# A last stage of two joined attentions: narrow heads in the text stage's form, wide keys and values on row tiles, keys first in the step

## The chip, the cores and the metric

The program runs on one core of a Trainium2 chip. The metric is the device time of one execution in microseconds (us), the median of several runs. The engines are named as the profile names them: PE (matmuls; PEld is its weight loads), DVE, ACT, POOL, and SP, which issues DMAs.

## The reference

`x` is 32 batches of 128 tokens by 128 features, `ctx_768` 32 batches of 128 tokens by 96. Four layers follow each other: L0 (layer norm, self attention, cross attention, gated feed-forward), L1 (narrow cross attention and feed-forward), L2 (wide cross attention) and L3 (narrow cross attention). The change concerns L2 and L3:

```python
# L2: 16 heads of 64
h = _layernorm(x, gamma, beta)
Q = (h @ Wq).reshape(B, NQ, 16, 64)
K = (context @ Wk).reshape(B, NC, 16, 64)
V = (context @ Wv).reshape(B, NC, 16, 64)
attn = softmax(einsum('bihd,bjhd->bhij', Q, K)) * 64 ** -0.5
x = x + einsum('bhij,bjhd->bihd', attn, V).reshape(B, NQ, 1024) @ Wo + bo
# L3: 16 heads of 8
q, k, v = x @ Wq.T, context @ Wk.T, context @ Wv.T        # 128 features
attn = softmax(einsum('bhqd,bhkd->bhqk', q, k) * 8 ** -0.5)
x = einsum('bhqk,bhkd->bhqd', attn, v) @ Wo.T + bo + x
```

All numbers are 32-bit floats. A batch needs nothing of another batch.

## The kernel before

The program has five stages, one behind the other, with a barrier after each: the two attentions of L0 (0 to 746 us), L0's feed-forward (to 858), L1's attention, called the text stage here (`text_attention`, L934, to 1031), L1's feed-forward (to 1099), and L2 with L3 in one stage (`wide_and_narrow`, L1266, to the end). `x` stays in SBUF throughout, and so does `ctxT`, the contexts turned so that features lie on partitions.

The last stage is a software pipeline over steps t of which each does one batch's worth of everything, for different batches. Each engine has its own list of a step's work, written by hand: PE's is `step` at L1629, ACT's at L1808, DVE's at L2017, POOL's at L2131, SP's behind L2157. In step t PE does, in this order: wide scores of batch t+1 in two halves (`w_score`, L1431; each half 32 passes on two row groups into two banks), weighing of the wide values of t-1 (`w_weigh`, L1518), half the queries and half the keys of t+2 (`project_T`, L1481), the first half of the transposes of the narrow probabilities of t-3 (`n_transpose_probs`, L1471), the wide output projection of t-1 (L1564), the narrow scores of t-2 (`n_score`, L1454), the other transposes, the transposed inverses (L1548), the other halves of queries and keys with the transposed narrow rows of t-1 between, the narrow weighing of t-3 (`n_weigh`, L1535), the narrow queries and keys of t-1, the transposed wide rows of t+3, the wide values of t+1 in two halves (`w_values`, L1507, 512 columns each) with the narrow output projection of t-3 between, and the narrow values of t-2.

Results of PE go through eight PSUM banks. Four (`scores`) hold the wide scores and, at other times of the step, the narrow ones. The other four are a ring: `order` (L1271) lists the 20 fills of a step as (name, batch offset, engine that empties it); the n-th fill of the program goes to bank n mod 4, and PE waits (`start_fill`, L1422) until the fill four places earlier has been emptied. So the order of this list, the order of PE's list and those of ACT and DVE must fit each other.

The softmax of a wide batch: DVE takes row maxima of a half's scores (L1882), ACT exponentiates the first eight heads head by head with the maximum as bias and sums on the way (`w_exponentiate_0`, L1686); for the other eight DVE subtracts and ACT exponentiates all at once (L1710), DVE sums. POOL multiplies by the inverse sums (`w_divide`, L2125). To turn the probabilities, DVE transposes them in squares of 32 by 32 (`w_turn_squares`, L1947), and SP moves the squares to DRAM and back to their turned places (`away` and `back`, L2160 and L2168, called the relay here). The narrow softmax has the same form with its own maxima, exponentials and sums, and PE turns its probabilities; the inverses are turned too and multiplied in as the weighed result is evicted.

Steps 4 to 27 are a loop of four steps each turn (`TURN`, L1277); the rest is written out. The last wide batch has its own step (L1587), with its probabilities turned by PE, and the steps after it a list of their own (`tail_step`, L1608).

The text stage does narrow attention of the same size (16 heads of 8) in another form, written out without a loop. Scores are computed twice: once with queries on partitions for the maxima alone (L1017, two matmuls of 256 columns per row group), and once turned, with keys on partitions (L1029, four of 128 columns), where the negated maxima, turned by PE (L1050) and appended to the queries by DVE (L1202, L1204), make the product come out less its maximum. ACT exponentiates the turned scores, four operations of 512 columns (L1126), and these are already in the form that the weighing (L1061) needs. A column of ones in the values gives the sums, and the division follows after the weighed result is turned back.

Loads of weights go through SP (`load`, L187); those of L2 are issued at the end of the first stage's program (`later_loads`, L226, at t == 2 * BATCHES), by `load_wide` (L199) in five DMAs of whole tensors.

## Time and profile before

| | us |
|---|---|
| median of 3 runs (lowest, highest) | 1674.45 (1668.0, 1679.09) |
| the profiled execution | 1676.32 |
| its span | 1674.6 |
| mean granted clock of TensorE | 0.99 |
| last stage | 1099 to 1674.6 |

Busy shares of the span: PE 97%, PEld 81%, DVE 75%, ACT 70%, POOL 42%. The span runs from the first to the last recorded instruction; the execution's own time is 1.7 us longer.

In rows of a timeline an entry holds consecutive instructions of one line and kind, with their number behind the x; its duration runs to the modelled end of the last, so that the next entry of the same engine can start a little before it ends. PEclk is the share of full speed that TensorE was granted.

### The profile page before, as it was taken

How to read it: one execution, taken by the hardware profiler on the slowest of the kernel's cores; microseconds unless marked ns; L12 is line 12 of the kernel's file. 1: busy time of each engine (PE TensorE's matmuls, PEld its weight loads, DVE VectorE, ACT ScalarE, POOL GpSimd, SP SyncE). 2: the span in 40 equal slices, each digit the busy share in tenths (PEclk: the TensorE clock that was granted, in tenths of full speed). 3: DMA queues.
4: the chain of work that ended last, by engine and by line, in shares of the span. 5: the costliest groups of instructions: out<-in, count | busy, mean ns of one | idle time of the engine just before them, and what ended most of it. 6: DMA issues, size and time to landing. Idle time of an engine off the chain costs nothing. (4 is left out here: it accounts for less than half of the span.)

```text
span 1674.6 us, 48052 instructions
## 1 busy us (share of the span) xinstructions
PE 1620.9 (97%) x16480; PEld 1348.4 (81%) x16480; DVE 1252.0 (75%) x2424; ACT 1174.7 (70%) x3648; POOL 704.6 (42%) x1027
## 2 busy tenths in 40 slices
PE   7999999999999999989999998988999999999998
PEld 5788888888888888879978887876888888888876
DVE  4877777777777777757767775656888888888885
ACT  4777777777777777743336665455888888888886
POOL 3444444454444444332224442643343444444441
PEclk9999999999999999999999999998999999999999
DMA  6777777788667776740000000014343444344440
GB/s 185 202 190 189 185 189 191 201 217 218 186 183 199 184 186 182 202 135 1 0 2 3 3 3 2 0 40 138 120 142 119 141 120 139 121 139 121 139 130 9
DMA packets 225246, 211.60 MB, mean 126 GB/s; under 512 B 19475, under 2 KB 222805, under 8 KB 225109
## 3 DMA queue, kind: packets, MB, share of 16 engines
q1 hardware_dynamic: 225108, 209.92, 45.4%
q8 instruction: 67, 1.10, 0.3%
q14 instruction: 71, 0.57, 0.1%
HBM read 109.72 MB, written 100.14 MB: 125 GB/s over the span
## 5 line engine op out<-in xcount | busy, mean ns | idle before, releaser
L907 POOL TENSOR_TENSOR L_probs<-L_probs,L_inv_sum 128x1024 f32<-128x1024 f32 x128 | 242.8, 1897 | 87.2 <-DVE L_inv_sum L803 87.2
L691 ACT ACTIVATE L_probs<-L_scores,L_neg_max 128x128 f32<-128x128 f32 x512 | 182.8, 386 | 135.0 <-DVE L_neg_max L783 135.0
L777 DVE TENSOR_REDUCE L_row_max<-L_scores 128x8 f32<-128x1024 f32 x128 | 156.2, 1220 | 41.8 <-PE L_scores L549 41.8
L2128 POOL TENSOR_TENSOR L2L_w_probs<-L2L_w_probs,L2L_w_inv_sum 128x1024 f32<-128x1024 f32 x64 | 121.4, 1896 | 124.2 <-DVE L2L_w_inv_sum L1931 123.7
L809 DVE STREAM_TRANSPOSE L_squares<-L_probs 128x1024 f32<-128x1024 f32 x125 | 153.0, 1224 | 0.3 <-POOL L_probs L907 0.3
L549 PE MATMUL L_scores<-L_kT,L_qT 64*128 64x128 f32 x2048 | 131.8, 278 | 0.9 <-ACT L_kT L680 0.9
L600 PE MATMUL L_ring<-L_probsT,L_v 128*64 128x128 f32 x2048 | 126.6, 276 | 3.9 <-issue 1.8
L600 PEld LDWEIGHTS L_ring<-L_probsT,L_v 128*64 128x64 f32 x2048 | 110.5, 137 | 23.9 <-issue 19.6
L549 PEld LDWEIGHTS L_scores<-L_kT,L_qT 64*128 64x128 f32 x2048 | 119.4, 188 | 12.5 <-ACT L_oT L680 8.1
L793 DVE TENSOR_REDUCE L_sums<-L_probs 128x8 f32<-128x1024 f32 x64 | 78.1, 1220 | 64.8 <-ACT L_probs L698 64.8
L1195 DVE TENSOR_REDUCE L_maxima<-L_s_banks 128x4 f32<-128x512 f32 x128 | 87.5, 688 | 44.6 <-PE L_s_banks L1017 44.6
L1695 ACT ACTIVATE L2L_w_probs<-L2L_scores,L2L_w_neg_max 128x128 f32<-128x128 f32 x256 | 90.4, 371 | 41.7 <-DVE L2L_w_neg_max L1895 41.7
L691 ACT ACTIVATION_READ_ACCUMULATOR L_probs<-L_scores,L_neg_max 128x1 f32 x512 | 115.8, 226 | 0.0
L680 ACT ACTIVATE L_oT<-L_ring 128x512 f32<-128x512 f32 x128 | 76.5, 599 | 39.7 <-PE L_ring L600 39.6
L1884 DVE TENSOR_REDUCE L2L_w_row_max<-L2L_scores 128x8 f32<-128x1024 f32 x64 | 76.7, 1198 | 28.8 <-PE L2L_scores L1450 28.8
L1706 ACT ACTIVATE L2L_n_probs<-L2L_scores,L2L_n_neg_max 128x128 f32<-128x128 f32 x256 | 90.7, 377 | 4.8 <-DVE L2L_n_neg_max L1901 4.1
L1253 POOL TENSOR_SCALAR L_k_apart<-L_qk,quad_mask 128x128 f32<-128x128 f32 x116 | 50.3, 448 | 93.2 <-ACT L_qk L1153 93.2
L680 ACT ACTIVATE L_kT<-L_ring 128x512 f32<-128x512 f32 x128 | 76.8, 600 | 18.2 <-PE L_ring L557 18.2
L2104 POOL TENSOR_TENSOR L2L_n_x_bias<-L2L_n_rows_h,bias_L 128x128 f32<-128x128 f32 x32 | 14.6, 456 | 177.9 <-DVE x L1980 177.8
L680 ACT ACTIVATE L_qT<-L_ring 128x512 f32<-128x512 f32 x128 | 76.2, 595 | 17.3 <-PE L_ring L557 12.0
L1126 ACT ACTIVATE L_exps<-L_t_banks 128x512 f32<-128x512 f32 x128 | 69.4, 597 | 19.7 <-PE L_t_banks L1029 19.7
L1684 ACT ACTIVATE L2L_n_probsT<-L2L_ring 128x512 f32<-128x512 f32 x128 | 70.4, 611 | 17.9 <-PE L2L_ring L1477 17.9
(236 smaller groups left out, 4578.7 us busy)
## 6 DMA issues: line engine op xcount, KB each, us to landing
L_relay<-L_squares SPq DMA_DIRECT2D x125, 512.0 KB, 3.4
L_probsT<-L_relay SPq DMA_DIRECT2D x500, 128.0 KB, 3.7
L2L_relay<-L2L_w_squares SPq DMA_DIRECT2D x62, 512.0 KB, 3.4
L2L_w_probsT<-L2L_relay SPq DMA_DIRECT2D x248, 128.0 KB, 2.9
out_x<-x SPq DMA_DIRECT2D x32, 64.0 KB, 2.7
L0a_wq<-in_L_xattn_Wq SPq DMA_DIRECT2D x2, 256.0 KB, 2.9
L0a_wk<-in_L_xattn_Wk SPq DMA_DIRECT2D x2, 256.0 KB, 3.2
L0a_wv<-in_L_xattn_Wv SPq DMA_DIRECT2D x1, 512.0 KB, 6.3
```

Source lines behind the costliest of these rows:

```text
L549: last = nc.tensor.matmul(scores[:, s, r, i, :], q[part, i, at.n % 2, :], k[part, i, at.n % 2, :], start=True, stop=True, tile_position=(h ...
L600: last = nc.tensor.matmul(to[WIDE * r:WIDE * (r + 1), TOKENS * i:TOKENS * (i + 1)], v[:, at.n % 2, WIDE * h:WIDE * (h + 1)], probsT[:, at. ...
L680: nc.scalar.activation(to, src, ACT.Copy).then_inc(emptied["act"], 1)
L691: done = nc.scalar.activation(slot_probs(at, 0)[:, n, :], scores[:, 0, r, i, :], ACT.Exp, scale=layer_of(at).scale, bias=neg_max[:, n:n + ...
L777: nc.vector.tensor_reduce(row_max[:, s, :], slot(s), AX.X, ALU.max).then_inc(max_ready[s], 1)
L793: nc.vector.tensor_reduce(sums[:, :, 1, :], slot_probs(at, 1).rearrange("p (r i) k -> p r i k", r=2), AX.X, ALU.add).then_inc(sum_ready, 1)
L809: nc.vector.transpose(squares[:, at.n % 2, :, SLOT_HEADS * s:SLOT_HEADS * (s + 1), :] .rearrange("p j h a -> p h j a"), slot_probs(at, s). ...
L907: nc.gpsimd.tensor_tensor(to, to, inv_sum[:, :, s, :].unsqueeze(3) .to_broadcast([TOKENS, 2, GROUP, TOKENS]), ALU.mult).then_inc(divided, 1)
L1195: nc.vector.tensor_reduce(maxima[:, b % 2, g, :, 0:1].rearrange("p j d -> p (j d)"), s_bank(b, g), AX.X, ALU.max, negate=True).then_inc(ma ...
L1695: done = nc.scalar.activation(w_slot(at, 0)[:, h, :], scores[:, 0, r, i, :], ACT.Exp, scale=W.scale, bias=w_neg_max[:, h:h + 1], accum_out ...
L1706: done = nc.scalar.activation(n_slot(at, 0)[:, h, :], scores[:, 0, r, i, :], ACT.Exp, scale=N.scale, bias=n_neg_max[:, h:h + 1], accum_out ...
L2128: nc.gpsimd.tensor_tensor(to, to, w_inv_sum[:, :, s, :].unsqueeze(3) .to_broadcast([TOKENS, 2, GROUP, TOKENS]), ALU.mult).then_inc(w_divid ...
```

## The change

- The stage is written out whole: no loop, no special last or tail steps. Where batch 31's probabilities are turned by PE, this stands at the front of step 32.
- The ring has 22 fills a step in another order, shown below.
- Wide keys and values are computed on row tiles. The 96 context features are three blocks of 32 rows, and the inner columns are split in four; each of PE's four row groups has one quarter of the columns, and adds up three products of 32 rows. For this the context lies four times in a new tile, `ctx_blocks` (one copy for each row group, 16 batches at a time), written to DRAM and loaded back by SP during the text stage, with later chunks of 8 batches loaded at steps 8 and 16. The weights lie in the same form, loaded in 24 DMAs instead of two. ACT empties keys and values as four copies of 256 columns each, where it made two of 512.
- In PE's list the keys of batch t+2 stand first, ahead of both halves of the wide scores of t+1.
- The narrow attention takes the text stage's form. Its scores are issued in two calls a step, `n_both_scores`; each interleaves the scores for the maxima of two row groups (batch t-2) with those less the maxima of the two other row groups (batch t-3).
- POOL sets the narrow parts (six operations of 128 columns), and takes the layer norm's normalisation from DVE; ACT takes the eviction of the turned wide rows from DVE. POOL no longer copies rows and contexts.
- At the stage's start DVE clears two tiles, 2,560 columns in all, where it cleared one of 1,280.

```diff
-    order = [("w.PV0", -1, "act"), ("w.PV1", -1, "act"), ("w.q0", 2, "act"), ("w.k0", 2, "act"),
-             ("n.T0", -3, "act"), ("n.T1", -3, "act"), ("w.Wo", -1, "dve"), ("n.T2", -3, "act"), ("n.T3", -3, "act"),
-             ("n.iT", -3, "act"), ("w.q1", 2, "act"), ("n.hT", -1, "act"), ("w.k1", 2, "act"), ("n.PV", -3, "dve"),
-             ("n.qk", -1, "act"), ("w.hT", 3, "dve"), ("w.v0", 1, "act"), ("n.Wo", -3, "dve"), ("w.v1", 1, "act"),
-             ("n.v", -2, "act")]
+    order = [*((f"w.k{g}", 2, "act") for g in CHUNKS_4), ("n.mT", -3, "dve"), ("w.PV0", -1, "act"),
+             ("w.PV1", -1, "act"), ("n.PV", -4, "act"), ("w.q0", 2, "act"), ("n.D", -4, "dve"), ("w.Wo", -1, "dve"),
+             *((f"w.v{g}", 0, "act") for g in CHUNKS_4), ("n.hT", -1, "act"), ("n.oT", -4, "act"),
+             ("w.q1", 2, "act"), ("n.qk", -1, "act"), ("n.v", -3, "act"), ("n.Wo", -4, "dve"), ("w.hT", 3, "act")]
...
+                for g in range(4):
+                    for r in range(CTX // 32):
+                        load(sp, "L2", W["L2", "k"][32 * g:32 * (g + 1), r, :, :], keys[g][:, r, :, :])
+                        load(sp, "L2", W["L2", "v"][32 * g:32 * (g + 1), r, :], values[g][:, r, :])
...
+            def n_both_scores(t, s_groups, t_groups):
+                for h in range(2):
+                    if real(t - 2):
+                        for g in s_groups:
+                            n_score_for_max(t - 2, g, h)
+                    if real(t - 3):
+                        for j in (2 * h, 2 * h + 1):
+                            for g in t_groups:
+                                n_score_less_max(t - 3, g, j)
...
+            def w_keys(b):
+                ctx_blocks.await_loaded(pe, b)
+                to = [start_fill(f"w.k{g}", b) for g in CHUNKS_4]
+                for c in range(2):
+                    for r in range(3):
+                        for g in CHUNKS_4:
+                            part = slice(QUAD * g, QUAD * (g + 1))
+                            last = nc.tensor.matmul(to[g][:, TOKENS * c:TOKENS * (c + 1)], W.wk[part, r, c, :],
+                                                    ctx_blocks.of(b)[part, r, :], start=r == 0, stop=r == 2,
+                                                    tile_position=(QUAD * g, 0))
...
+            def w_values(b):
+                to = [start_fill(f"w.v{g}", b) for g in CHUNKS_4]
+                for r in range(3):
+                    for g in CHUNKS_4:
+                        part = slice(QUAD * g, QUAD * (g + 1))
+                        last = nc.tensor.matmul(to[g][:, 0:INNER // 4], ctx_blocks.of(b)[part, r, :], W.wv[part, r, :],
+                                                start=r == 0, stop=r == 2, tile_position=(QUAD * g, 0))
```

PE's list of a step after, without the tests of whether a batch exists:

```diff
+            for t in range(first, last + 1):
+                    w_keys(t + 2)
+                    w_score(t + 1, 0)
+                    w_score(t + 1, 1)
+                    n_transpose_maxima(t - 3)
+                    w_weigh(t - 1, 0)
+                    w_weigh(t - 1, 1)
+                    n_weigh(t - 4)
+                    w_queries(t + 2, 0)
+                    n_turn_back(t - 4)
+                    w_project_out(t - 1)
+                n_both_scores(t, (0, 1), (2, 3))
+                    w_values(t)
+                n_both_scores(t, (2, 3), (0, 1))
+                    n_transpose_h(t - 1)
+                    n_transpose_o(t - 4)
+                    w_queries(t + 2, 1)
+                    n_queries_keys(t - 1)
+                    n_values(t - 3)
+                    n_project_out(t - 4)
+                    w_transpose_h(t + 3)
```

The lists of ACT and DVE follow suit. ACT's: four copies of keys, exponentials of the first four heads, copies of the weighed wide values (two of 512 columns), of `n.PV` and `w.q0`, exponentials of the next four heads and of the second half (1024 columns), two narrow exponentials of 512 columns, four copies of values, `n.hT`, `n.oT`, two narrow exponentials, `w.q1`, `n.qk`, `n.v`, `w.hT`. DVE's: row maxima of half 0, their negation, inverses, row maxima of half 1, the subtraction, the append of the narrow maxima (which empties `n.mT`), squares, statistics, the narrow division (empties `n.D`), the wide finish, inverses, narrow maxima of two groups, sums, narrow maxima of two groups, squares, the narrow finish. The waits of PE's new parts:

```diff
+            def w_score(b, s):
+                await_emptied(pe, f"w.q{s}", b)
+                if s == 0:
+                    for g in CHUNKS_4:
+                        await_emptied(pe, f"w.k{g}", b)
+                    if real(b - 4):
+                        pe.wait_ge(n_max_ready, 4 * (b - 4) + 4)
...
+                elif real(b - 5):
+                    pe.wait_ge(n_exp_ready, 4 * (b - 5) + 4)
...
+            def n_score_for_max(b, g, h):
...
+                    if g >= 2:
+                        pe.wait_ge(n_max_ready, 4 * b + g - 1)
+                    elif real(b + 3):
+                        pe.wait_ge(w_exp_ready[0], 2 * (b + 3) + 2)
...
+            def n_score_less_max(b, g, j):
...
+                    await_emptied(pe, "n.mT", b)
+                    if g < 2:
+                        pe.wait_ge(n_exp_ready, 4 * b + g + 1)
+                    elif real(b + 4):
+                        pe.wait_ge(w_shifted, b + 5)
```

## Rows read from the trace of the kernel before

**Rows 1.** Windows of the last stage: head, 26 steps, tail, a stretch of the head.
```profile
core 0: us, PE busy (x) PEld busy (x) DVE busy (x) ACT busy (x) POOL busy (x), PEclk, DMA share, GB/s
1101.00:1183.06 82.06, 70.26 (x620) 56.04 (x618) 53.26 (x98) 50.78 (x173) 30.03 (x44) 0.92 0.34 103
1183.06:1617.54 434.48, 431.87 (x4758) 363.40 (x4757) 374.85 (x644) 380.40 (x1327) 183.71 (x258) 1.00 0.44 131
1617.54:1674.60 57.06, 45.99 (x507) 36.18 (x506) 33.95 (x59) 40.99 (x139) 13.44 (x18) 0.94 0.14 42
1160.40:1167.20 6.80, 6.52 (x23) 4.24 (x25) 3.25 (x5) 4.75 (x17) 1.33 (x2) 0.50 0.52 157
```

**Rows 2.** Timeline of PE, one steady step: start, duration, engine, line, operation, operands.
```profile
1417.39 2.06 PE L1450 MATMUL L2L_scores<-L2L_w_kT,L2L_w_qT 64*128 64x128 f32 x32
1419.38 1.97 PE L1529 MATMUL L2L_ring<-L2L_w_probsT,L2L_w_v 128*64 128x128 f32 x32
1421.27 1.16 PE L1484 MATMUL L2L_ring<-L2L_w_hT,L_wq 128*128 128x128 f32 x8
1422.27 1.06 PE L1484 MATMUL L2L_ring<-L2L_w_cT,L_wk 96*128 96x128 f32 x8
1423.16 1.04 PE L1477 MATMUL L2L_ring<-ident,L2L_n_probs 128*128 128x128 f32 x8
1424.04 1.95 PE L1569 MATMUL L2L_ring<-L_wo,L2L_w_oT 128*128 128x128 f32 x16
1425.92 1.14 PE L1467 MATMUL L2L_scores<-L2L_n_k_apart,L2L_n_qT 32*128 32x512 f32 x8
1426.99 1.09 PE L1477 MATMUL L2L_ring<-ident,L2L_n_probs 128*128 128x128 f32 x8
...
1430.02 1.08 PE L1542 MATMUL L2L_ring<-L2L_n_probsT,L2L_n_v 128*32 128x128 f32 x32
1431.15 0.48 PE L1503 MATMUL L2L_ring<-L2L_n_hT,L_wqT 128*128 128x128 f32 x2
...
1431.81 1.02 PE L1509 MATMUL L2L_ring<-L_wv,L2L_w_cT 96*128 96x512 f32 x2
1432.66 0.39 PE L1575 MATMUL L2L_ring<-L_woT,L2L_n_oT 128*128 128x128 f32 x2
```

**Rows 3.** Timeline of PE in the text stage, from the turned maxima on.
```profile
944.39 0.33 PE L1050 MATMUL L_b_bank<-ident,L_maxima 128*128 128x128 f32 x1
944.64 1.08 PE L1061 MATMUL L_a_bank<-L_exps,L_v 128*32 128x128 f32 x32
945.66 0.48 PE L1017 MATMUL L_s_banks<-L_k_apart,L_q_part 32*128 32x256 f32 x2
...
946.22 0.39 PE L1029 MATMUL L_t_banks<-L_q_part,L_k_apart 32*128 32x128 f32 x4
...
946.44 0.39 PE L1029 MATMUL L_t_banks<-L_q_part,L_k_apart 32*128 32x128 f32 x4
946.76 0.33 PE L1074 MATMUL L_a_bank<-ident,x 128*128 128x128 f32 x1
```

**Rows 4.** Groups by line, text stage, weight loads: busy us, mean ns, idle before.
```profile
L1029 PEld LDWEIGHTS L_t_banks<-L_q_part,L_k_apart 32*128 32x128 f32 x864 | 52.6, 186 | 0.3 <-issue 0.2
```

**Rows 5.** Timeline of DVE, text stage and the steady step of rows 2.
```profile
945.05 0.34 DVE L1202 SCALAR_TENSOR_TENSOR L_q_part<-L_b_bank,L_half_mask,L_q_part 128x128 f32<-128x128 f32 x1
...
945.57 0.68 DVE L1195 TENSOR_REDUCE L_maxima<-L_s_banks 128x4 f32<-128x512 f32 x1
...
1418.60 1.23 DVE L1884 TENSOR_REDUCE L2L_w_row_max<-L2L_scores 128x8 f32<-128x1024 f32 x1 [0.78 <-PE L2L_scores L1450]
```

**Rows 6.** Timeline of ACT in the same step.
```profile
1420.17 0.37 ACT L1695 ACTIVATE L2L_w_probs<-L2L_scores,L2L_w_neg_max 128x128 f32<-128x128 f32 x1 [1.02 <-DVE L2L_w_neg_max L1895]
...
1421.55 1.09 ACT L1684 ACTIVATE L2L_w_oT<-L2L_ring 128x512 f32<-128x512 f32 x2
```

**Rows 7.** Waits of SP's queue, 690 to 780 us: in total, times, longest.
```profile
SPq L385 <- PEq L385: 10.8, 1, 10.8
```

**Rows 8.** Timeline of SP at the end of the first stage, one issue of a load.
```profile
733.31 0.43 SPq L187 DMA_DIRECT2D L_wq<-in_L_xattn_Wq  x1
```

1153 lines of the change are left out of this document (471 added, 682 removed).

## The prediction

> **What bounds the kernel now.** I read the table of windows first, one row per stretch of the last stage [rows 1]. Its row from 1183.06 to 1617.54 us runs from the wide scores that step 4 issues to those of step 30, so it holds 26 steps: 434.48 / 26 = 16.71 us each. PE is busy for 431.87 of the 434.48, DVE for 374.85, ACT for 380.40, POOL for 183.71. So PE alone sets the step, and the other engines keep up with it. Then the timeline of PE over one of these steps [rows 2]: groups follow each other without a gap, and from start to start the scores take 1.99 us, the weighing of wide values 1.89, a half of the queries 1.00, a half of the keys 0.89, two fills of transposed narrow probabilities 0.88, the wide output projection 1.88, the narrow scores 1.07, the narrow weighing 1.13, half of the wide values 0.85. Eight passes of 128 columns in 0.88 make 0.11 a pass. The head of the stage (82.06 us) has PE busy for 70.26 at a mean clock of 0.92, with stretches such as 1160.40 to 1167.20 at 0.50, the 1.2 GHz level; the tail takes 57.06 us [rows 1].
>
> The profiled execution took 1676.32 us (span 1674.6), the median of the three runs is 1674.45. The sum is made against 1676.32; at the median's level everything stands 2 us lower. A measurement of this kernel tells about 1% (17 us) from no change.
>
> **What leaves PE in a step** [rows 2]: four fills of narrow transposes 2 x 0.88, the transposed inverses (one pass, 0.11), keys 2 x 0.89, values 2 x 0.85, narrow scores 1.07, narrow weighing 1.13: 7.55.
>
> **What comes.** The text stage already runs the narrow form that is taken over, and its timeline prices it [rows 3]: transposed maxima 0.25, weighing 1.02 (944.64 to 945.66), one call of both kinds of scores 1.10 (945.66 to 946.76), of which the change issues two: 2.20. Turning back is two passes, 0.22, turning the output one, 0.11. Wide values by row tiles are 12 matmuls of 256 columns; as a matmul is two passes (the 4 of a half of the queries stand as x8), this is 24 passes in 6 sets of four row groups, each at twice 0.11: 1.30. Wide keys are 24 matmuls of 128 columns, 48 passes in 12 sets. No row shows this shape. If a set costs one pass it is 12 x 0.11 = 1.32, and nothing goes below that. By the text stage's weighing (32 passes on four tiles at a time in 1.02, 0.032 a pass) it is 1.53. By a call of both scores (24 passes on four row groups in 1.10, 0.046 a pass) it is 2.2. I take 1.42, between the two nearest, and keep 2.2 for the range. Another change of tile shape costs 0.1 (the narrow weighing of before took 1.13, the text stage's 1.02). Sum: 0.25 + 1.02 + 2.20 + 0.22 + 0.11 + 1.30 + 1.42 + 0.1 = 6.6. PE's work falls by about 1 us a step, to 15.5 where each group is counted on its own.
>
> How weights come in decides about the keys. In a call of both scores the scores less maxima run on two row groups, x4 at 946.22 and x4 at 946.44 [rows 3]: two passes for each row group in 0.22, though one load of weights there lasts 186 ns [rows 4]. So a row group takes its next weights at the pace of its passes. The Trainium skill, "TensorE: Matmul & The Clock Gate", Part 3 (The mechanism, what overlaps and what doesn't), says that a weight load overlaps running matmuls only when its row group differs; with all four row groups busy, as in the new keys, each set would then wait for its own loads. These rows don't bear that out for two row groups of four; for a set on all four no row here speaks. What it would make of the time is the third rival.
>
> **What then waits.** I walked a steady step in order: each engine's list as the diff has it, durations of rows, 0.2 us from PE's last pass to its reader (half of the scores is done 1.0 after 1417.39, and the reduce of it starts at 1418.60 [rows 2, 5]), about 0.1 between other engines; neighbours on an engine overlap a little, so on ACT 512 columns cost 0.48, 256 some 0.27, four exponentials with sums 1.38 (1420.17 to 1421.55 [rows 6]). Time 0 is the first half of the wide scores.
> - Scores end at 1.99, transposed maxima at 2.18, wide weighing at 4.08, narrow weighing at 5.1. The queries then want the bank of the transposed maxima, four fills back. DVE appends those only behind both row maxima and the subtraction: 1.25 + 1.26 + 0.23 + 1.20 + 1.14 = 5.08, and the append is two operations, 0.6 [rows 5]. PE waits 0.6.
> - Queries from 5.7, turning back, output projection to 8.85. The first call of both scores needs ACT's second half of the exponentials, behind the copy of the queries: 0.1. After the values the second call waits for the maxima of the first two groups, two reduces of 0.61 to 0.68 on DVE [rows 5]: 0.25.
> - The transpose of the next wide rows goes to the bank of the second half of the queries. ACT copies that behind four copies of values, two turned blocks and two exponentials of 512 columns, until about 14.8: 0.3.
> - The keys stand first in the next step and want the last four banks at once. The latest is that transpose's, which ACT empties behind two other copies: 0.5. Nothing of PE's lies between the two, so nothing covers it.
>
> Work 15.5 and waits 1.75 give a step of 17.25 us. With the keys at 1.32 the walk gives 17.15, at 1.53 17.35, at 2.2 about 18.0. Its softest term is the handoff: with none at all the step is 16.4, with handoffs half as long again 17.8.
>
> **Other engines.** ACT loses the narrow exponentials' accumulations and the copies of turned probabilities and comes to 10.9 us a step in the walk, DVE to 11.8, POOL to 8.2 (it takes over the normalisation and sets the narrow parts): below the step, so they matter by their order alone. The relay through DRAM starts from DVE's squares as before; in the walk a landing 2 us later moves nothing. Twice in the steady steps SP issues a chunk of context, 12 x 0.43 = 5 us [rows 8], between relays: inside that slack or nearly, 0 to 3 us each; I take 0.
>
> **Before the stage.** At the end of the first layers SP issues 22 more loads: 22 x 0.43 = 9.5 us [rows 8], against 10.8 that SP waited there for PE [rows 7]. I take 0; if pieces issue more slowly than whole tensors, up to 6 show. The text stage gets one write and 24 loads on an SP without other work: 0.
>
> **Head and tail.** The walk gives the head 76 us, with memsets of 2,560 columns ahead of the first statistics (the 1024-wide reduce takes 1.23 [rows 5], so about 1.5 more than for the 1,280 columns of before). Of the 82.06 at a mean clock of 0.92, some 6.6 are lost clock [rows 1]. The new head idles too, so I let half of that come back: -3 (-7 to +1). In the tail the last batch's turned probabilities stay about the same work and the narrow chain is one lag longer: +3 (0 to +5).
>
> **Sum**: 26 x (17.25 - 16.71) = +14, -3, +3: +14 on 1676.3, at the median's level 1674.45 + 14 = 1688.5, so 1689.
>
> **Rivals.**
> - *Packed PE.* The waits come from my handoffs, and ACT and DVE run early enough. For it: PE was packed before and is packed in the text stage [rows 2, 3]. Against: the append can't pass the subtraction in DVE's list. A step of 15.6: 26 x (15.6 - 16.71) = -29, head -3, tail +3: 1645. With waits of half the size (16.4): 1668.
> - *Keys at the rate of single passes, slower.* At 0.046 a pass, as in both scores, the keys take 2.2, all of it bare at the step's front: 18.0, +34: 1708. It decides where the group takes over 1.9. For it: the row of both scores; against: the row of the weighing [rows 3].
> - *Keys waiting for their loads, slower.* A set's loads start when its row groups are free: 12 x (0.186 + 0.11) = 3.6 [rows 3, 4], a step of 19.4, +70: 1746. Against: the beat of 0.22 above. This is the Trainium skill's rule of "TensorE: Matmul & The Clock Gate", Part 3.
> - *Clock.* Waits now recur in every step, and in the head (11.8 us of idle in 82) rows at 0.50 follow [rows 1]. A drop of 3.4 us in each step costs 1.7: +44 more, 1733. Against: each new wait is at most 0.6.
> - *It doesn't do what it says.* The row groups run one after another, so keys and values cost 48 x 0.11 and 24 x 0.22, 10.6 instead of 2.7: past 1850. Against: the call of both scores [rows 3].
>
> **Chances.** Forecast with its handoffs (1672 to 1705): 0.57. Packed or half packed: 0.16. Keys at the rate of single passes: 0.17. Waiting for loads 0.03, clock 0.06, no overlap 0.01. The likeliest is 1689. To hold 8 in 10 the range goes from 1658 (takes in the half-packed case) to 1712 (the keys at 2.2). Slower by over 1% (over 1691.2): the last four rivals, 0.27, and the upper part of the forecast's own range, 0.15: 0.42. Faster by over 1% (under 1657.7): most of the first rival, 0.14. Within 1%: 0.44.
>
> **What would show it.** In the profile of the changed kernel: 17.25 us from scores to scores; PE busy near 90% of the steady window where it was 99%; idle ahead of the first queries laid to DVE's append (0.6), ahead of the keys to ACT's copy of the turned rows (0.5), and ahead of that transpose (0.3); the keys 1.3 to 1.5 from start to start. The walk is wrong if PE is packed, the tiles' price if the keys take 2 us, and the rest if the first layers end later or the steady window's clock is under 1.00.

## The result, and the profile after

| | before | after |
|---|---|---|
| median of 4 runs each, us | 1674.43 | 1714.74 |
| lowest to highest | 1668.0 to 1679.09 | 1711.64 to 1719.87 |
| ratio after to before, 95% interval | | 1.0246 (1.0213 to 1.028) |
| the profiled execution / its span | 1676.32 / 1674.6 | 1719.87 / 1718.1 |

The change makes the kernel slower by 2.5%, 40 us. The forecast was 1689, the range ended at 1712. The windows of the last stage after, cut at the same events as [rows 1] (head from the first statistics to the wide scores of step 4, 26 steps, tail):

```profile
core 0: us, PE busy (x) PEld busy (x) DVE busy (x) ACT busy (x) POOL busy (x), PEclk, DMA share, GB/s
1111.44:1191.70 80.26, 63.58 (x926) 56.67 (x925) 45.65 (x81) 47.22 (x161) 37.69 (x55) 0.94 0.36 112
1191.70:1651.12 459.42, 419.47 (x6767) 383.02 (x6763) 306.97 (x565) 314.31 (x1012) 223.17 (x331) 1.00 0.44 131
1651.12:1718.10 66.98, 55.79 (x717) 46.30 (x716) 25.31 (x57) 28.93 (x81) 18.65 (x33) 0.84 0.13 40
```

459.42 / 26 = 17.67 us a step; all but the last (14.98) and one other (18.48) are 17.75 (the forecast: 17.25, before: 16.71). PE is busy for 91% of it where it was 99%, at a full clock. The profiled execution is the slowest of the four, 5 us over their median. Against the profile of before its 43.5 us of span come from: the 26 steps +24.9, the tail +9.9, the head -1.8 with 0.7 more ahead of it, and 9.7 before the last stage begins, where the rest of the program is the same. Half of these 9.7 stand at the barrier after the first layers, half in the feed-forward behind it. The first 14 us of that feed-forward, before and then after:

```profile
746.00:760.00 14.00, 11.46 (x69) 10.21 (x70) 9.13 (x34) 5.27 (x10) 3.55 (x8) 1.00 0.01 1
```

```profile
751.00:765.00 14.00, 11.85 (x41) 10.24 (x42) 5.61 (x24) 3.26 (x6) 3.56 (x8) 0.53 0.14 43
```

It starts 4.9 us later (751.34 for 746.45), and then runs at a clock of 0.53, so that 41 passes are done where before there were 69. Of the 4.9 us, 1.9 are that PE's last projection ahead of the barrier starts later (745.67 for 743.74), and 3.0 that PE then waits 3.6 us where it waited 0.7. SP's timeline shows what it waits for: a load of a piece of weights, with its strides, is issued in 0.57 to 0.68 us, one in 1.11 (two stand for 24), where [rows 8] had 0.43 for a whole tensor. The 24 take 15.5 us, from 734.29 to 749.84, and SP's own wait at the barrier, 10.8 us in [rows 7], is 0.2:

```profile
734.29 0.68 SPq L188 DMA_DIRECT2D L_wk<-in_L_xattn_Wk  x1
735.02 0.58 SPq L188 DMA_DIRECT2D L_wv<-in_L_xattn_Wv  x1
```

```profile
SPq L404 <- PEq L404: 0.2, 1, 0.2
```

One steady step on PE after, to be read against [rows 2] (in brackets the idle time before an entry, and what ended it):

```profile
1421.57 1.62 PE L1509 MATMUL L2L_ring<-ctx_blocks,L_wk 32*128 32x128 f32 x48 [0.64 <-ACT L2L_w_hT L1718]
1423.12 2.06 PE L1445 MATMUL L2L_scores<-L2L_w_kT,L2L_w_qT 64*128 64x128 f32 x32
1425.11 0.33 PE L1567 MATMUL L2L_ring<-ident,L2L_n_maxima 128*128 128x128 f32 x1
1425.36 1.97 PE L1536 MATMUL L2L_ring<-L2L_w_probsT,L2L_w_v 128*64 128x128 f32 x32
1427.26 1.08 PE L1579 MATMUL L2L_ring<-L2L_n_exps,L2L_n_v 128*32 128x128 f32 x32
1428.88 1.13 PE L1497 MATMUL L2L_ring<-L2L_w_hT,L_wq 128*128 128x128 f32 x8 [0.54 <-ACT L2L_n_weighed L1669]
1429.85 0.38 PE L1590 MATMUL L2L_ring<-ident,L2L_n_weighed 128*128 128x128 f32 x2
1430.07 1.95 PE L1556 MATMUL L2L_ring<-L_wo,L2L_w_oT 128*128 128x128 f32 x16
1432.18 0.48 PE L1460 MATMUL L2L_scores<-L2L_n_k_apart,L2L_n_q_part 32*128 32x256 f32 x2 [0.17 <-ACT L2L_w_probs L1680]
...
1435.95 0.33 PE L1596 MATMUL L2L_ring<-ident,x 128*128 128x128 f32 x1
...
1437.79 0.39 PE L1617 MATMUL L2L_ring<-L_woT,L2L_n_oT 128*128 128x128 f32 x2
1438.38 0.30 PE L1562 MATMUL L2L_ring<-ident,L2L_w_rows_h 128*128 128x128 f32 x1 [0.20 <-ACT L2L_w_qT L1669]
1439.32 1.62 PE L1509 MATMUL L2L_ring<-ctx_blocks,L_wk 32*128 32x128 f32 x48 [0.64 <-ACT L2L_w_hT L1718]
```

The group of keys takes 1.55 us from start to start (1421.57 to 1423.12): 48 passes, 0.032 each, though their weight loads last 186 ns each:

```profile
L1509 PEld LDWEIGHTS L2L_ring<-ctx_blocks,L_wk 32*128 32x128 f32 x1200 | 36.5, 186 | 20.1 <-issue 20.1
```

The waits stand where the walk put them: ahead of the queries, of the first call of both scores, of the wide rows' transpose and of the keys. The bracket counts from the modelled end of the pass before; from start to start, less the passes themselves, the four are 0.60, 0.23, 0.37 and 0.83 us (the last is 1439.32 less 1438.38 and a pass of 0.11). The last is the large one. On ACT, the chain behind it:

```profile
1436.32 0.28 ACT L1669 ACTIVATE L2L_n_hT<-L2L_ring 128x128 f32<-128x128 f32 x1 [0.49 <-PE L2L_ring L1596]
...
1436.65 1.10 ACT L1690 ACTIVATE L2L_n_exps<-L2L_scores 128x512 f32<-128x512 f32 x2
1437.60 0.63 ACT L1669 ACTIVATE L2L_w_qT<-L2L_ring 128x512 f32<-128x512 f32 x1
1438.08 0.43 ACT L1669 ACTIVATE L2L_n_qk<-L2L_ring 128x256 f32<-128x256 f32 x1
1438.34 0.34 ACT L1669 ACTIVATE L2L_n_v<-L2L_ring 128x128 f32<-128x128 f32 x1
1438.72 0.46 ACT L1718 ACTIVATE L2L_w_hT<-L2L_ring,L_ln_b,L_ln_g 128x128 f32<-128x128 f32 x1
```

ACT works without a gap from the exponentials to the copy of the narrow values; the copy of the wide rows, with scale and bias, takes 0.46, where the plain copies of 128 columns take 0.28 (`n.hT`) and 0.34 (`n.v`). And ahead of the queries, on DVE (the profile names ACT's `n_weighed` for that wait, which is not in the list of what these queries wait for; the append ends at 1428.73, 0.15 before them):

```profile
1426.99 1.23 DVE L1805 TENSOR_TENSOR L2L_w_probs<-L2L_scores,L2L_w_row_max 128x1024 f32<-128x1024 f32 x1
1428.13 0.34 DVE L1846 SCALAR_TENSOR_TENSOR L2L_n_q_part<-L2L_ring,L2L_half_mask,L2L_n_q_part 128x128 f32<-128x128 f32 x1
1428.39 0.34 DVE L1848 SCALAR_TENSOR_TENSOR L2L_n_q_part<-L2L_ring,L2L_half_mask,L2L_n_q_part 128x128 f32<-128x128 f32 x1
```

### The profile page after: what moved, and what is told of

Its sections match the earlier page's. It is cut to its first block and busy times, and to the rows that moved or that the text cites. A ratio compares the mean times of both kernels' runs of the same rounds, so it can differ in the third digit from the quotient of the medians.

```text
span 1718.1 us, 51406 instructions
## 1 busy us (share of the span) xinstructions
PE 1619.2 (94%) x19008; PEld 1384.8 (81%) x19008; DVE 1168.3 (68%) x2330; ACT 1093.2 (64%) x3264; POOL 757.0 (44%) x1126
## 5 line engine op out<-in xcount | busy, mean ns | idle before, releaser
L1840 DVE TENSOR_REDUCE L2L_n_maxima<-L2L_scores 128x4 f32<-128x512 f32 x128 | 82.4, 686 | 31.0 <-PE L2L_scores L1460 31.0
L699 ACT ACTIVATE L_qT<-L_ring 128x512 f32<-128x512 f32 x128 | 76.2, 595 | 16.2 <-PE L_ring L576 10.8
L1690 ACT ACTIVATE L2L_n_exps<-L2L_scores 128x512 f32<-128x512 f32 x128 | 69.7, 602 | 25.9 <-PE L2L_scores L1476 25.9
L1497 PE MATMUL L2L_ring<-L2L_w_hT,L_wq 128*128 128x128 f32 x512 | 70.7, 282 | 14.9 <-ACT L2L_n_weighed L1669 13.4
L1460 PE MATMUL L2L_scores<-L2L_n_k_apart,L2L_n_q_part 32*128 32x256 f32 x512 | 77.7, 396 | 6.4 <-ACT L2L_w_probs L1680 4.4
```

The costliest lines, as they stand in the source:

```text
L699: nc.scalar.activation(to, src, ACT.Copy).then_inc(emptied["act"], 1)
L1460: last = nc.tensor.matmul(s_bank(g)[:, 2 * (1 - h):2 * (1 - h) + 2, :], n_q_part[part, b % 2, h, :], n_k_apart[part, b % 2, 2 * h:2 * h + ...
L1497: last = nc.tensor.matmul(to[:, TOKENS * c:TOKENS * (c + 1)], W.wq[:, BANK * n + 128 * c:BANK * n + 128 * (c + 1)], w_hT[:, b % 2, :], sta ...
L1690: nc.scalar.activation(n_exps[:, b % 2, GROUP * g:GROUP * (g + 1), :].rearrange("p h q -> p (h q)"), t_bank(g).rearrange("p j q -> p (j q) ...
```

## The experiments

Each kernel is the changed one with the edit named, unless said otherwise. "Step" is the usual time from wide scores to wide scores in the trace, "tail" from the scores of the last wide batch to the end. The kernel before was run again beside each group, and the ratios are to it: 1675.42 us beside the first four experiments, 1671.91 beside the next four, 1675.52 beside the next three, 1675.29 beside the last three. So whole times of different groups can stand 3.6 us apart by that alone. Tails and heads are from one profile each.

**The 24 loads moved into the text stage.**

```diff
         def first_context_blocks(sp):
...
+            for g in range(4):
+                for r in range(CTX // 32):
+                    load(sp, "L2", W["L2", "k"][32 * g:32 * (g + 1), r, :, :], keys[g][:, r, :, :])
+                    load(sp, "L2", W["L2", "v"][32 * g:32 * (g + 1), r, :], values[g][:, r, :])
             ctx_blocks.write(sp, ctxT)
```

> Edit: the 24 loads of the wide weights' row tiles are issued by SP at the start of the text stage, where SP has nothing else to do, in place of the end of the first stage. Theory A (SP's issue time holds the barrier after the first stage by 4.9 us, and the idle PE then starts the feed-forward at half clock, 4.8 us more): the feed-forward's first statistics come back to 746.4 us from 751.3, its first 20 us run at a clock of 1.00, and the whole is 9 to 10 us shorter than the changed kernel, near 1705. Rival B (the loads themselves, 24 short transfers, collide with the feed-forward): the barrier comes 4.9 us earlier, the other 4.8 us move to the text stage, near 1710. Rival C (the clock drop there is chance): 4.9 us and no more.

Measured: 1710.03 us, ratio 1.0206 (1.0183 to 1.0229), step 17.75. The feed-forward starts at 745.0 and its first 14 us run at full clock:

```profile
745.00:759.00 14.00, 11.89 (x73) 10.63 (x74) 9.40 (x37) 5.25 (x10) 3.56 (x8) 1.00 0.00 1
```

So the loads held the barrier. In all six profiles with the loads in the old place SP waits 0.2 us there and PE 3.4 to 4.9; in the ten others, the kernel before among them, SP waits 10.7 to 14.3 and PE 0.7. What the clock adds is not settled. From the feed-forward's first statistics to the text stage's first memset the changed kernel's profile shows 98.9 us, and 94.1 is the time at full clock. The five others with the loads in the old place show 95.2 to 95.9. But so do four of the ten that have no such wait, 95.6 to 95.8, among them the kernel with four edits below:

```profile
750.00:764.00 14.00, 11.90 (x58) 10.20 (x59) 7.95 (x30) 5.21 (x10) 3.56 (x8) 0.88 0.00 1
```

So up to 1.7 us are lost there without the wait too, and the 4.8 that theory A adds stand in one profile only. The last stage begins 11.1 us earlier than in the changed kernel's profile, where theory A wanted 9 to 10, but the medians differ by 4.7, and the intervals of the two ratios overlap. For the whole that is nearer to rival C.

**The wide rows turned earlier.** PE's transpose, ACT's copy and the ring's entry move together:

```diff
-             ("w.q1", 2, "act"), ("n.qk", -1, "act"), ("n.v", -3, "act"), ("n.Wo", -4, "dve"), ("w.hT", 3, "act")]
+             ("w.hT", 3, "act"), ("w.q1", 2, "act"), ("n.qk", -1, "act"), ("n.v", -3, "act"), ("n.Wo", -4, "dve")]
```

> Edit: the transpose of the wide rows of batch t+3 and its copy stand ahead of the second half of the queries, no longer at the end of the step; the ring's list follows. Theory A (the keys wait bare for the chain transpose, copy on ACT, release, 0.94 us from transpose to keys, and the transpose itself waits 0.37 for the bank of the queries): the keys then wait for the copy of the narrow values and for DVE's last operation alone, some 0.3 to 0.5 us after PE's last projection; the step falls from 17.75 to 17.0 to 17.2, the whole by 15 to 23 us. Rival B (ACT's list as a whole is late at the end of the step, whatever stands last): the wait stays with another name, the step within 0.2 of 17.75. Rival C (the keys are slow because of their weight loads): the group of keys keeps 1.55 us, as in A, so B and A are told apart by the step alone.

Measured: 1712.42 us, step 17.70. Rival B. The wait ahead of the transpose is gone, but the keys now wait 1.0 us by the bracket, where it was 0.64, and for another copy, the last one that ACT makes:

```profile
1431.82 0.39 PE L1617 MATMUL L2L_ring<-L_woT,L2L_n_oT 128*128 128x128 f32 x2
1433.19 1.62 PE L1509 MATMUL L2L_ring<-ctx_blocks,L_wk 32*128 32x128 f32 x48 [0.99 <-ACT L2L_n_v L1669]
```

Here the keys wait for the last copy of ACT's list, whichever it is.

**The append earlier on DVE.**

```diff
+                if real(t - 3):
+                    n_append_maxima(t - 3)
                 if real(t + 1):
                     w_row_maxima(t + 1, 1)
                     w_subtract_maxima(t + 1)
-                if real(t - 3):
-                    n_append_maxima(t - 3)
```

> Edit: in DVE's list the append of the narrow maxima stands ahead of the second row maxima and the subtraction. Theory A (the queries wait 0.54 us for the bank that this append empties): that wait is gone, and what hangs on it follows; the step falls by 0.4 to 0.55 us to 17.2 to 17.35, the whole by 11 to 14 us. Rival B (the profile's name for that wait, ACT's copy of the narrow weighed values, is the true one): the wait of 0.54 stays and the step with it, at 17.75. Rival C (the subtraction, 0.5 us later, delays the second exponentials and with them the narrow scores): the gain is given back at the first call of both scores, whose idle time grows from 0.17 to 0.6.

Measured: 1701.36 us, ratio 1.0151 (1.0126 to 1.0176), step 17.17, shorter by 0.58 (two steps are longer, 18.02 and 18.04). The waits of PE over 1187.8 to 1633.8 us (in total, times, longest) no longer have the queries (L1497), and the other three are as they were:

```profile
PE L2L_ring L1509 <- ACT L2L_w_hT L1718: 16.0, 25, 0.6
PE L2L_ring L1562 <- ACT L2L_w_qT L1669: 5.0, 25, 0.2
PE L2L_scores L1460 <- ACT L2L_w_probs L1680: 4.5, 26, 0.2
```

Theory A, with a gain just over its range; the releaser that the profile named was not the true one.

**Keys and values at full height**, the rest as changed:

```diff
...
+            def w_keys(b):
+                for n in range(2):
+                    to = start_fill(f"w.k{n}", b)
+                    for c in range(4):
+                        last = nc.tensor.matmul(to[:, TOKENS * c:TOKENS * (c + 1)],
+                                                W.wk[0:CTX, BANK * n + 128 * c:BANK * n + 128 * (c + 1)],
+                                                ctxT[0:CTX, b, :], start=True, stop=True)
...
```

> Edit: wide keys and values at full height again (96 rows, two fills of 512 columns each, straight from the turned contexts), in the same places of the step; the narrow form and the rest stay as changed, and the loads, the blocks of contexts and their DMAs go. Theory A (row tiles save PE little and cost waits: keys on four row groups want four banks at once): PE's work grows by 0.3 for the keys and 0.4 for the values, the keys' wait of 0.64 goes (their banks are those of narrow projections, emptied earlier), so the step comes to 17.4 to 17.8, and the 9.7 us ahead of the stage come back: 1695 to 1707 in all. Rival B (row tiles are the cause of the longer step): the step falls under 17.0, the whole under 1690. Rival C (row tiles are what keeps the step short): the step is over 18.2.

Measured: 1709.65 us, step 17.98: between the forecasts, and the whole just over theory A's 1695 to 1707. The wait ahead of the keys is gone, yet the step is 0.23 longer, so PE's work grew by more than the 0.7 expected; the row tiles do shorten the step. The whole is not longer, since the first layers end without delay (745.8) and the head takes 73.8 us, 6.5 less. What shortens the head by so much was not tried.

**The last two exponentials at the end of ACT's list.**

```diff
-                if real(t - 3):
-                    n_exponentiate(t - 3, 0)
-                    n_exponentiate(t - 3, 1)
                 if real(t + 2):
                     w_queries(t + 2, 1)
...
                     w_turned_h(t + 3)
+                if real(t - 3):
+                    n_exponentiate(t - 3, 0)
+                    n_exponentiate(t - 3, 1)
```

> Edit: on ACT the last two narrow exponentials of a step (512 columns each) stand at the end of its list, behind the copies of the second queries, the narrow projections and the wide rows. The earlier transposing of the wide rows left the step at 17.71 us and the keys waiting 1.0 us for the last copy on ACT, so theory A now reads: ACT's list from these exponentials on is the chain that ends last, whatever is copied last. It predicts that the copy of the queries starts some 0.4 us earlier, PE's transpose of the wide rows no longer waits, and the keys start 0.35 us earlier: a step of 17.3 to 17.45, the whole 8 to 11 us shorter than the changed kernel. Rival B (the handoff transposes, copy, keys alone sets it, 0.94 us after the transpose whenever that comes): the step stays over 17.65. Rival C (the exponentials are missed by the next narrow weighing or the next scores): a new wait there of 0.3 us or more, and a step over 17.75.

Measured: 1709.07 us, step 17.43, shorter by 0.32, and the wait ahead of the transpose is gone: the step follows theory A. The medians fell by 5.7 only. In the profiles, 10.9 us apart, the 26 steps give 8.4, while the tail is 1.2 longer (68.2) and the head 2.7; the rest lies ahead of the stage, where the two kernels are the same.

**Keys behind both halves of the wide scores.**

```diff
-                if real(t + 2):
-                    w_keys(t + 2)
                 if real(t + 1):
                     w_score(t + 1, 0)
                     w_score(t + 1, 1)
+                if real(t + 2):
+                    w_keys(t + 2)
```

> Edit: the keys stand behind both halves of the wide scores in PE's list, and their copies on ACT behind the exponentials of the first four heads; the ring's list stays. Theory A (at the front of the step nothing covers the keys' wait): the scores follow the last projection without it, the keys find their four banks empty, and the wait of 0.64 us goes; a new one comes behind the keys, where the transposed maxima want the first keys' bank, which ACT empties only behind the exponentials (0.4 to 0.9). Step 17.0 to 17.4. Rival B (the place of the keys is worth nothing, what is won at the front is lost there in full): 17.65 to 17.85. Rival C (the front was the better place): over 17.9.

Measured: 1710.22 us, step 17.64: Rival B, a hair under its range. The wait at the front is gone, and the transposed maxima behind the keys wait for the copy of the keys (now behind the exponentials on ACT):

```profile
1412.13 1.62 PE L1509 MATMUL L2L_ring<-ctx_blocks,L_wk 32*128 32x128 f32 x48
1414.73 0.30 PE L1567 MATMUL L2L_ring<-ident,L2L_n_maxima 128*128 128x128 f32 x1 [0.98 <-ACT L2L_w_kT L1669]
```

The place of the keys is worth 0.1 us a step as long as the lists of ACT and DVE stay.

**Four edits at once**: the loads, the earlier append, the earlier transpose of the wide rows, the late exponentials.

> Edit: four at once: the 24 loads in the text stage, the earlier append, the wide rows' transpose ahead of the second queries, and the two exponentials at the end of ACT's list. Theory A (waits of ACT's and DVE's order make the step longer than before, PE's own work is 15.6): without the wait for the append and without ACT's late chain the step is 16.2 to 16.8, and the whole, with 5 to 10 us for the loads, 1668 to 1685. Rival B (PE's own work is longer than 15.6, the waits hide behind it): the step stays over 17.0 with no wait left that is worth naming. Rival C (a new chain, through the narrow exponentials or the relay, takes over): over 17.0 with one wait of more than 0.5 us.

Measured: 1684.1 us, ratio 1.0058 (1.0038 to 1.0078), step 16.61: theory A. Alone the three edits of order gave 0.58, 0.05 and 0.32, or 0.95, together 1.14. That the transpose is worth more once ACT's list no longer ends late would explain the rest; no run leaves it out of the three, so this is not shown. PE's waits, 1300 to 1600 us, two of them:

```profile
PE L2L_ring L1509 <- DVE x L1863: 8.6, 18, 0.5
PE L2L_scores L1460 <- ACT L2L_w_probs L1680: 3.1, 18, 0.2
```

Two steps of the 26 are longer, 17.64 and 18.24. Its tail:

```profile
1616.86:1686.00 69.14, 56.78 (x717) 46.87 (x716) 25.43 (x57) 29.98 (x82) 18.74 (x33) 0.81 0.13 39
```

**As that, with products of the identity in the tail** (`keep_clock(nc, to[:, 0:TOKENS], ident, 2)`, or 4, on the bank that is filled next, ahead of the waits of turning back, weighing, turning the output and projecting).

> Edit: as the kernel with four edits, and in the narrow parts of the last five batches PE multiplies the identity with itself (two or four products, into a bank that it fills next) ahead of four waits. It adds work whose result is overwritten. Theory A (the tail's 67 us, against 57 before, hold some 12 us of half clock from about 35 us before the end, where before it was 3.4): with PE kept busy the half-clock stretches shrink to some 10 us and the tail is 4 to 8 us shorter than that of the kernel without. Rival B (the tail is a chain of handoffs between ACT, DVE and PE, and the clock matters little to it): the clock rises and the time stays within 2 us. Rival C (the added products lie on the chain): 2 to 6 us longer.

Measured: 1688.39 us. The clock of the tail rises from 0.81 to 0.98, and the tail is 70.3 us against 69.1: inconclusive, since the 128 added passes, at 0.11 us each, take about 14 us on PE, in part in place of waits (its busy time in the tail grows by 7.3).

**The narrow finish ahead of the squares on DVE**, on top of the four edits:

```diff
+                if real(t - 4):
+                    n_finish(t - 4)
                 if real(t + 1) and t + 1 != LAST_WIDE:
                     w_turn_squares(t + 1, 0)
-                if real(t - 4):
-                    n_finish(t - 4)
```

> Edit: the kernel with four edits, and in DVE's list the narrow finish, which empties the bank of the narrow output projection, stands ahead of the last squares of the step. Theory A (with four edits the keys still wait 0.5 us, now for this bank, which DVE empties behind squares of 1.24 us): the finish comes 0.3 us earlier, the keys with it, the step falls from 16.72 to 16.35 to 16.5, the whole by 6 to 10 us against the four edits' 1684. Rival B (ACT's copy of the narrow values comes as late): the wait changes its name and the step stays over 16.65. Rival C (the squares, and with them the relay, come too late): a wait of the weighing of wide values for the landing.

Measured: 1687.88 us. The usual step stays at 16.61 and the wait ahead of the keys at 0.5: theory A falls. It is the handoff from the last projection through DVE to the keys, which want that bank and have nothing ahead of them. Rival C came in part: two steps are 20.9 and 22.4 us long. SP issues 12 loads of context in one go, and the relay of the next squares stands behind them; with the four edits alone the same loads cost 1.0 and 1.6 us, and here the last squares of the step also start later (0.2 us ahead of the keys, where it was 1.9). SP's timeline, and PE's at the second of the two:

```profile
1394.38 6.47 SPq L2035 DMA_DIRECT2D ctx_blocks<-ctx_turned  x12
1400.95 0.52 SPq L1983 DMA_DIRECT2D L2L_relay<-L2L_w_squares  x1
```

```profile
1410.03 1.97 PE L1536 MATMUL L2L_ring<-L2L_w_probsT,L2L_w_v 128*64 128x128 f32 x16 [2.87 <-issue]
```

Of the 5.8 us by which that step is too long, 2.9 are this wait; behind it PE is busy and runs at a mean clock of 0.58 from 1410 to 1417 us, which makes about the other half (an estimate: 7.0 x 0.42 = 2.9). In the changed kernel, with its longer step, the loads show once, as a step of 18.48 us.

**A last wide step of its own**, on top of that: the last batch's turned probabilities, weighing and output projection come in step 31 instead of 32.

```diff
+                if t == LAST_WIDE:
+                    w_transpose_probs(t, 0)
+                    w_transpose_probs(t, 1)
...
+                if t == LAST_WIDE:
+                    w_weigh(t, 0)
+                    w_weigh(t, 1)
...
+                if t == LAST_WIDE:
+                    w_project_out(t)
```

> Edit: as the kernel before it in this call, with a last wide step of its own: the last batch's probabilities are turned by PE at the end of step 31, its weighing, output projection and finish follow there, and its narrow rows are turned at the front of step 32; in the changed kernel all this stands in step 32. Theory A (the tail of 67 to 70 us against 57 is a chain of handoffs of the last batch that starts a step late; the clock that falls meanwhile is its consequence, as holding the clock changed nothing): the tail shrinks to 57 to 62 us and the whole by 7 to 12 us against the kernel before it. Rival B (the narrow form's own last steps, max, append, second scores, exponentials, division, are the tail): it stays over 65. Rival C (step 31 is so full that it gives back what is won): step 31 longer by more than 6 us, the whole within 3 us.

Measured: 1691.3 us, tail 72.1: not A, and over 65 as rival B has it. The last wide finish on DVE comes 31.4 us into the tail instead of 34.2 (first the kernel without this step, then with it):

```profile
1657.56 0.29 DVE L1835 SCALAR_TENSOR_TENSOR x<-L2L_ring,L2L_w_x_bias 128x128 f32<-128x128 f32 x1 [1.21 <-PE L2L_ring L1556]
```

```profile
1652.09 0.29 DVE L1855 SCALAR_TENSOR_TENSOR x<-L2L_ring,L2L_w_x_bias 128x128 f32<-128x128 f32 x1 [6.19 <-PE L2L_ring L1562]
```

But the last three narrow finishes then follow 11.0, 10.6 and 6.1 us apart, at half clock, where without this step they followed 8.5, 7.5 and 6.0 apart. Tail windows of the kernel without and with this step:

```profile
1623.32:1687.50 64.18, 51.21 (x717) 41.83 (x716) 26.32 (x58) 29.73 (x82) 18.64 (x33) 0.93 0.14 42
```

```profile
1620.69:1692.80 72.11, 59.89 (x717) 48.91 (x716) 26.35 (x58) 30.05 (x82) 18.65 (x33) 0.76 0.12 37
```

**Full height with these edits** (append, transpose, exponentials, finish, last wide step; no later loads).

> Edit: wide keys and values at full height, with the other edits: the earlier append, the earlier transpose of the wide rows, the late exponentials, the earlier finish and the last wide step; the loads are those of the kernel before the change. Theory A (with the waits gone, PE's own work decides, and the row tiles save 0.2 to 0.6 us of it a step): the step is 16.5 to 16.9, longer than that of the kernel with row tiles and the same edits by 0.2 to 0.5; but the head is 4 to 6 us shorter and no loads hold the first stage's end, so the whole is within 6 us of that kernel. Rival B (the row tiles cost their gain by waits): the step is shorter than with row tiles, the whole 8 us or more below it. Rival C: the step is over 17.2.

Measured: 1685.98 us, step 16.92, head 71.9, tail 71.0. Theory A, with a step just over its range. Here PE is packed again, 433.63 of 438.03 us, at the longer step:

```profile
1172.36:1610.39 438.03, 433.63 (x5444) 371.98 (x5443) 305.12 (x564) 309.93 (x906) 224.16 (x331) 1.00 0.43 130
```

This kernel shows what the row tiles are worth. Its PE at both calls of scores with the values between, then at the keys:

```profile
1400.84 0.48 PE L1456 MATMUL L2L_scores<-L2L_n_k_apart,L2L_n_q_part 32*128 32x256 f32 x2 [0.17 <-ACT L2L_w_probs L1676]
...
1405.16 0.33 PE L1584 MATMUL L2L_ring<-ident,x 128*128 128x128 f32 x1
...
1407.33 2.01 PE L1502 MATMUL L2L_ring<-ctxT,L_wk 96*128 96x128 f32 x16
1409.27 2.06 PE L1441 MATMUL L2L_scores<-L2L_w_kT,L2L_w_qT 64*128 64x128 f32 x32
```

The keys take 1.94 us here and 1.55 on row tiles, the stretch of scores and values 4.32 and 3.77: row tiles save 0.94 us of PE's time in a step. Of this 0.64 goes back, the wait of the keys for their last bank that stays with the four edits (1417.29 to 1418.15 there, less two passes of 0.11); at full height they start without a wait. What is left is the 0.31 between 16.92 and 16.61.

**The clock of the tail, with products that fit into waits.** On the four edits with the last wide step and with the context loads spread two to a step (1); on full height with the same edits, without the earlier finish (2); on the changed kernel alone (3):

```diff
+            def hold(to, b):
+                if b >= BATCHES - 4:
+                    keep_clock(nc, to[:, 0:TOKENS], ident, 2)
...
+                hold(to, b)
                 await_emptied(pe, "n.PV", b)
```

(1) 

> Edit: the kernel with four edits and the last wide step of its own; the 24 later loads of context blocks go two to a step over six steps, no longer twelve in one; and in the narrow parts of the last four batches PE multiplies the identity with itself twice ahead of three waits (0.44 us each, overwritten), where PE waits 0.4 to 0.5 anyway. Theory A (in the kernel with the last wide step the clock was at half for the last 36 us and a narrow-only step took 10.9 us, where at full clock it took 7.5 in the kernel with the earlier finish): the clock stays at 1.00 for most of the tail, the narrow-only steps take 7.5 to 8.5 us, the tail is 57 to 63 us where it was 72, and the two long steps (20.9 and 22.5 us among 16.61) are gone: 1664 to 1674 in all. Rival B (the narrow-only steps are handoffs and the clock is not their cause): the clock holds and the tail stays over 67. Rival C (the clock falls all the same): tail over 70, clock at 0.5.

(2) 

> Edit: the kernel with keys and values at full height and the other edits (without the earlier finish), with the same products of the identity ahead of three waits in the last four batches. Theory A: the tail falls from 71 to 57 to 63 us, the step stays at 16.6 to 16.9, the whole comes to 1668 to 1678. Rival B (handoffs, not the clock): the tail stays over 67, the whole over 1682.

(3) 

> Edit: the changed kernel with nothing but these products of the identity in the last four batches. Theory A (of the 10 us by which the changed kernel's tail is longer than before, 4 to 6 are lost clock, the rest the narrow form's chain): the tail is 61 to 64 us where it was 67, the whole 3 to 6 us shorter than the changed kernel. Rival B (all of it is clock): 57 to 59. Rival C (all of it is the chain): 66 to 69 at a clock near 1.

Measured: (1) 1677.72 us, ratio 1.001 (0.9996 to 1.0023): no longer told apart from before. No step is long any more (16.61 to 16.66, the last 14.40; 429.83 for 26), so the two long steps of the four edits came from the context loads issued in one go. (This kernel also has the narrow finish behind the squares again.) (2) 1680.8, ratio 1.0036 (1.0023 to 1.0049). (3) 1714.44, no gain. The three tails:

```profile
1608.18:1675.00 66.82, 57.42 (x765) 49.17 (x764) 25.42 (x57) 30.07 (x82) 18.64 (x33) 0.94 0.14 40
```

```profile
1610.98:1676.50 65.52, 56.36 (x725) 45.97 (x724) 25.74 (x58) 29.84 (x78) 18.73 (x33) 0.97 0.14 41
```

```profile
1646.24:1714.90 68.66, 59.97 (x765) 51.64 (x764) 25.30 (x57) 28.75 (x81) 18.73 (x33) 0.90 0.13 39
```

In (3) the clock rose from 0.84 to 0.90 and the tail went from 67.0 to 68.7: Rival C by the time, but not at a clock near 1, and the products themselves take PE's time (busy 60.0 us for 55.8), so clock and chain are not told apart. In (1) and (2) the tail lies between A and B: 5 us shorter than without the products (72.1 and 71.0), still 65 to 67. No kernel of the study beats the one before.

## Why the prediction was wrong

**What bounds the kernel, and PE's work: right.** The step's work came out at 17.75 less waits of 2.3 = 15.45, the forecast 15.5. The keys took 1.55 (1.42 and 0.1 for the shape), next to the bound by the weighing's row, 1.53.

**The waits: right in place, too small in sum.** This is the step that failed first, and the largest single miss: 1.75 us a step forecast, 2.3 measured. Ahead of the queries 0.6 and 0.60; the first call 0.1 and 0.23; in the values and the second call together 0.25 and 0.27 (1432.18 to 1435.95 is 3.77, passes 3.5); the transpose 0.3 and 0.37; the keys 0.5 and 0.83. The keys are most of the miss. The prediction shows no price for ACT's copy of the turned wide rows; with 0.2 and 0.1 for the handoffs its 0.5 leaves room for a plain copy of 128 columns (0.28 to 0.34) at best, and this copy, with scale and bias, took 0.46. That is only half of it: turned earlier, the rows freed nothing, for ACT's list ended as late with another copy. Two edits of order, on DVE and on ACT, took 0.58 and 0.32 us off the step, with the transpose 1.14. In the profile the steps are 11 us of the 29 that the forecast missed.

**The loads before the stage: sized wrongly.** 22 x 0.43 = 9.5 us were to hide behind 10.8; the 24 issues took 15.5, and PE waited 3.4 to 4.9 us at the barrier in the six profiles with these loads, where it waited 0.7 before. That lies within the "up to 6" that the text set as its bound, and not at the 0 that it took. What the text did not see is that the feed-forward behind the barrier can start at half clock: 4.8 us more in the changed kernel's profile, 1.1 to 1.9 in five others with the same loads; since up to 1.7 were also lost without the wait, how much of this the loads cause stays open.

**Head and tail.** The head gave -1.8 and what stands ahead of it +0.7, for -3. The tiles that are cleared there are 256 and 1,536 columns wide in the trace, 1,792 in all and not the 2,560 of the section on the change, and clearing them took 0.9 us more than before, not 1.5. The tail gave +9.9 for +3. Up to the end of the last wide finish it is 33.8 us for 32.7, so 8.8 of the 9.9 lie behind that, where the last four narrow finishes follow 5.8 to 9.9 us apart. Both the clock and the order of the work take part. From step 30 on the kernels with four edits and with the earlier finish run the same instructions, and their tails are 69.1 us at a clock of 0.81 and 64.2 at 0.93: 5 us, with the clock as the one difference that the windows show, from one profile each. Between 64.2 at 0.93 and the 57.1 of before at 0.94 there are still 7 us, which these mean clocks do not explain. The chain of the last batches through maxima, append, second scores, exponentials and division is the likely cause; no run takes a part of it out. Starting the last wide work a step earlier did not help: the last wide finish came 2.8 us sooner and the end 7.9 later, at 0.76. For the changed kernel itself (67.0 at 0.84) the two shares stay open, since the products that held the clock cost time of their own.

**The rivals.** Packed PE was wrong for this order, and half right as a direction: with other lists the step was 16.61, not the 15.6 of PE's own sum. The keys at the rate of single passes did not come (1.55, not 2.2). Nor did the keys waiting for their loads, 3.6: 12 sets on all four row groups took 0.13 us each, with loads of 186 ns. So the rule of the Trainium skill ("TensorE: Matmul & The Clock Gate", Part 3) that loads overlap only passes of another row group is not borne out by these rows, unless they are the other case that the same Part names, loads into the background weight buffer. The row groups did not run one after another either, which would have made 10.6 us of keys and values. The steady window ran at 1.00: waits of up to 0.83 us, four in a step, cost no clock there. Two of the rivals' totals, 1668 and 1746, were added to the profile's time and not to the median like the others; they stand 2 us too high. In the sum, the forecast's sign was right and its size a third: +14 for +40 by the medians. By the profiles it is +43.5, and of the 29 us that are missing the steps make 11, the stretch ahead of the stage 10, the tail 7 and the head 2.

## What to carry to other kernels

A bound engine that is relieved by 1 us of 16.7 does not give it back by itself: as soon as its work is under the period, the order of the other engines' lists decides, and here it took more than was saved. Before a group goes to the front of a step, ask which copy its buffers wait for and how late that engine's list ends; one that wants four buffers at once waits for the last of them bare. And count the DMAs that a new layout needs where they are issued: on a queue with 10 us to spare, 24 strided issues cost 15.5, and twelve in one go stood ahead of a relay. And compare the clocks of two tails before their times: the same instructions took 64 and 69 us here.

## What the runs showed of the hardware

- Issuing a load of a strided piece of a weight took SP 0.57 to 0.68 us (once 1.11), where a whole weight took 0.43.
- 48 passes of 128 columns on four row groups in turn ran at 0.032 us each, the pace of the weighing's four column tiles; full-height passes take 0.11.
- On ACT a plain copy of 128 columns took 0.28 to 0.34 us, the same with scale and bias 0.46.
- In six profiles PE had waited 3.4 to 4.9 us at the barrier, and the next 14 us ran at 0.54 to 0.88 of the clock; in ten it had waited 0.7, and they ran at 1.00 in six and at 0.88 in four. Behind a wait of 2.9 us in the steady steps PE ran at a mean clock of 0.58 for the next 7 us; waits of 0.2 to 0.83 us four times in each 17.75 us step left it at 1.00.
- The same instructions in the tail took 69.1 us at a mean clock of 0.81 and 64.2 at 0.93.
- The profile's releaser for the queries' wait (ACT) was not the one: moving an operation of DVE removed it.
